# Fifth layer: the bias reaches the rows through the residual instead of through a product

## What is computed

```python
def _sage_conv(x, src, dst, Wl, b, Wr):
    agg = segment_sum(x[src], dst, num_segments=n)
    cnt = segment_sum(ones, dst, num_segments=n)
    mean = agg / jnp.maximum(cnt, 1.0)[:, None]
    return mean @ Wl + b + x @ Wr

x = _layernorm(x + L0(x))    # layers 1 and 2, 128 -> 128 -> 128, relu between
x = _layernorm(x + L1(x))    # layers 3, 4, 5: 128 -> 256 -> 256 -> 128, relu between
```

## Time and profile before

| what | us |
|---|---|
| median of three runs (5212.83 to 5214.96) | 5212.95 |
| the profiled execution, own time | 5213.1 |
| its span | 5211.5 |
| PE busy in the span | 4970.9 (95%) |
| DVE / ACT / POOL busy | 3692.6 / 2554.6 / 2342.6 |
| last pass (b3), first to last bias product | 4032.2 to 5196.4 |

### The profile page before, as it was taken

One profiled execution on the slowest core, in us unless ns is written; L12 is line 12 of the kernel. 1 busy time (PEld: TensorE's weight loads), 2 busy tenths in 40 slices (PEclk: granted clock), 3 DMA queues, 4 the chain that ended last, 5 costly groups with the idle time before them and its releaser, 6 DMA issues. The chain is left out here.

```text
span 5211.5 us, 156564 instructions
## 1 busy us (share of the span) xinstructions
PE 4970.9 (95%) x42398; PEld 4907.3 (94%) x42399; DVE 3692.6 (71%) x10002; ACT 2554.6 (49%) x7254; POOL 2342.6 (45%) x2947
## 2 busy tenths in 40 slices
PE   1899989999998999999899999999998999999999
PEld 0788889999998999999899999999998999999999
DVE  4688877888887999999666666767675555555555
ACT  0455547777774333333333333333333666666666
POOL 1788866666644444444332323222222444444441
PEclk9999999999998999999999999999999999999999
DMA  1677777888875655665555555555555766666665
GB/s 29 172 211 210 208 198 210 229 229 228 229 224 160 196 193 196 197 196 194 167 173 179 173 179 173 178 174 178 174 177 162 222 216 219 219 217 219 219 216 186
DMA packets 1247576, 1007.06 MB, mean 193 GB/s; under 512 B 70406, under 2 KB 1178275, under 8 KB 1247492
## 3 DMA queue, kind: packets, MB, share of 16 engines
q1 hardware_dynamic: 1171780, 825.23, 51.2%
q0 software_dynamic: 75712, 180.76, 11.4%
HBM read 645.58 MB, written 360.13 MB: 193 GB/s over the span
## 5 line engine op out<-in xcount | busy, mean ns | idle before, releaser
L1206 PE MATMUL f_product_b<-f_ring_b,f_onehot_b 128*128 x6272 | 997.2, 281 | 0.0
L1206 PEld LDWEIGHTS f_product_b<-f_ring_b,f_onehot_b 128*128 128x128 f32 x6272 | 856.3, 189 | 0.0
L778 PE MATMUL m_product_a<-m_ring_a,m_onehot_a 128*128 x4704 | 846.9, 291 | 0.0
L1262 ACT ACTIVATE f_ring_b<-f_e_product_b,t_rec_all 128x256 f32 (+1 forms) x784 | 329.4, 471 | 1010.0 <-PE f_e_product_b L1219 1010.0
L1200 PE MATMUL f_product_b<-b_r_all,f_t_hi_b 128*128 128x256 f32 x2352 | 723.1, 307 | 0.0
L901 DVE TENSOR_TENSOR m_onehot_b<-iota_all,t_win_all 128x512 f32<-128x512 f32 x392 | 269.6, 688 | 557.3 <-PE m_product_b L778 557.3
L1202 PE MATMUL f_product_b<-b_r_all,f_t_lo_b 128*128 128x256 f32 x2352 | 661.2, 281 | 0.0
L1201 PE MATMUL f_product_b<-b_r_all,f_t_hi_b 128*128 128x256 f32 x2352 | 659.6, 280 | 0.0
L778 PEld LDWEIGHTS m_product_a<-m_ring_a,m_onehot_a 128*128 128x128 f32 x4704 | 651.9, 192 | 0.0
L1139 POOL TENSOR_TENSOR f_held_b<-ones_all 1x1 f32<-1x1 f32 x390 | 71.5, 183 | 1243.0 <-ACT f_e_idx_b L1244 1152.6
L901 DVE TENSOR_TENSOR m_onehot_a<-iota_all,t_win_all 128x512 fp32r<-128x512 f32 (+1 forms) x784 | 536.8, 686 | 102.7 <-PE m_product_a L778 94.0
(11 more groups left out here) (197 smaller groups left out, 12292.7 us busy)
## 6 DMA issues: line engine op xcount, KB each, us to landing
g<-f_rows_out_b SPq DMA_DIRECT2D x392, 512.0 KB
f_rows_in_b<-g SPq DMA_DIRECT2D x196, 512.0 KB, 4.1
m_rows_in_b<-g SPq DMA_DIRECT2D x196, 512.0 KB
m_t_full_a<-in_x_flat_dram SPq DMA_DIRECT2D x196, 256.0 KB
h<-m_rows_out_a SPq DMA_DIRECT2D x196, 256.0 KB
m_rows_in_a<-h SPq DMA_DIRECT2D x196, 256.0 KB
m_res_in_a<-in_x_dram SPq DMA_DIRECT2D x196, 256.0 KB, 3.1
x<-m_rows_out_a SPq DMA_DIRECT2D x196, 256.0 KB
```

Of the source, the lines that this page charges most:

```text
L778: mm = pe.matmul(both, onehot[:, s, n, :], ring[:, bass.ds(at[n] * (C * fo), C * fo)], start=False, stop=(w == 1), skip_group_check=True)
L1206: mm = pe.matmul(to, onehot[:, s, n, :], ring[:, bass.ds(at[n] * (2 * fo) + half * fo, fo)], start=False, stop=(w == 1 and half == 1))
```

## The change

In the pass of b3 alone (`biased=True`), the bias product is not issued; the first product by Wr of a group carries `start=True`. POOL adds the bias to the residual rows in place, once per group, behind the step's gathers; DVE's `add_up` waits for that addition (new semaphore `s_biased`) instead of for the residual's DMA. The other four passes are as they were.

```diff
@@ pool @@
+            def add_bias(g):
+                s = g.slot(2)
+                wait(pool, res_here[s], g.turn(2) + 1)
+                pool.tensor_tensor(res_in[:, s, :, :], res_in[:, s, :, :],
+                                   cv["bias"][:, :].unsqueeze(1).to_broadcast([P, T, P]),
+                                   ALU.add).then_inc(s_biased.sem, 1)
...
                     gather(p.plus(D))
                 if norm and split and has(g, 1):
                     mix(g.plus(-1))
+                if biased and g is not None:
+                    add_bias(g)
@@ tensor @@
-                    if norm and not split:
+                    if norm and not split and not biased:
                         pe.matmul(product[s][:, :], pr.two_rows[:, :],
...
-                                  start=(not norm and not split and t == 0 and k == 0), stop=False,
+                                  start=(not split and (biased or not norm) and t == 0 and k == 0), stop=False,
@@ vector, add_up @@
-                        wait(v, res_here[s], g.turn(2) + 1)
+                        if biased:
+                            wait(v, s_biased, g.n(1))
+                        else:
+                            wait(v, res_here[s], g.turn(2) + 1)
@@ build @@
-            dict(name="b3", h=g2, out=o2, relu=True, w=2, f_out=128, turned=False, Wl=b_wl3, Wr=b_wr3, b=b_b3,
+            dict(name="b3", h=g2, out=o2, relu=True, w=2, f_out=128, turned=False, biased=True, Wl=b_wl3, Wr=b_wr3, b=b_b3,
```

More of the change, by code:

```diff
@@ L571, in narrow_pass @@
     shared = cv.get("shared", 0)
+    biased = cv.get("biased", False)
     R = 3 if flat is not None else 2
@@ L609, in narrow_pass @@
         names = ("turned", "full", "onehot", "product", "sum", "stats", "meanvar", "std", "rstd", "shift", "normed",
-                 "index", "held", "eturned", "efull", "eproduct", "ring", "ringhi", "part", "mixed", "rest", "eps")
+                 "index", "held", "eturned", "efull", "eproduct", "ring", "ringhi", "part", "mixed", "rest", "biased", "eps")
         (s_turned, s_full, s_onehot, s_product, s_sum, s_stats, s_meanvar, s_std, s_rstd, s_shift, s_normed,
          s_index, s_held, s_eturned, s_efull, s_eproduct, s_ring, s_ringhi, s_part, s_mixed,
-         s_rest, s_eps) = [pr.counter("m_" + x) for x in names]
+         s_rest, s_biased, s_eps) = [pr.counter("m_" + x) for x in names]
         s_done = s_normed if norm else s_sum
@@ L1040, in narrow_pass @@
         s_rest.passed(G)
+    if biased:
+        s_biased.passed(G)
     if norm:
```

## The result

The median fell from 5213.95 to 5171.78 us (4 runs each, 5170.79 to 5172.64 after): ratio 0.9918, 95% interval 0.9901 to 0.9935, 42.2 us less. The prediction said 5170.9. The profiled execution took 5171.59 us with a span of 5169.9.

A forecast was written before the change was run, and what follows sets the result against it. PE was taken to bound the kernel. From the profiled 5213.1 us, 45.1 saved and 3.1 added at the pass's start gave 5171.1, as a median 5170.9 us; the range was 5166 to 5178.

The forecast's parts named there:

- The price of the product: On PE in the last pass: leaving the bias product out saves 0.23 us a step, 45.1 us, between 43 and 47.
- 216 ns: The skill's time for an isolated matmul of 512 columns; the prediction said the trace agrees with it, not the sustained 131 ns.
- The addition: On POOL, once per step: 128x512 values were put at 1.2 us, with bounds of 0.66 and 1.94 us.
- The steady step: POOL holds 4.5 of 5.77 us with the new work, so it costs nothing there and PE does not wait.
- The start: Start of the last pass: POOL has 26 gathers first, so PE waits 2.9 us at group 2; 3.1 us in all.
- I add 0.2 for both: Start of the last pass: 0.2 us for late residual loads behind DVE's sum and ACT's late copy of edge rows.
- The rows of group 4: Residual load behind DVE's late first sum: lands at 4051.2 to 4051.7, PE wants it at 4051.6, a tie.
- Rival 1: PE's clock falls in the new gap at the pass's start, losing 3 to 5 us: 5174 to 5176; chance 0.15.
- Rival 2: The bias product was partly overlapped on PE, at 131 ns, so the time is 5190 us; chance 0.03.
- rival 3: A wait at the first product by Wr replaces the saving, 0.23 us idle a step: 5216 us; chance 0.04.
- Rival 4: POOL's serial list becomes the bound, deciding from an addition of 2.5 us; at 3.5 us, 5360 us; chance 0.04.
- if POOL's idle time is gone: A sign in the profile after that would show the prediction wrong; it expected idle time still ahead of each POOL marker.

## Why the prediction was right

- **The price of the product**: 0.23 us a step and 45.1 us were forecast; leaving it out (with the addition gone) measured 45.2 us, doubling it 45.8. The reading of starts, not durations, carried it: the duration, 476 ns, would have said 93 us. The stated error of 43 to 47 us was too narrow: two distances of starts are subtracted and one of them is doubled, so 0.01 us in each start can add up to 0.06 us a step, 12 us in all.
- **The figure of 131 ns for a sustained matmul of 512 columns** from the Trainium skill, TensorE: Matmul & The Clock Gate, section on the back-to-back issue gap, does not hold here: a second such matmul put right behind the first adds 0.234 us a step. The prediction's reason for preferring the section's 216 ns, a distance of 0.31 us to the next start, fits neither figure; the price of 0.231 to 0.234 us is what lies near it.
- **The addition**: 1.2 us from IOTA's slope, 1.28 measured. The factor of two of the Trainium skill (GPSIMD Engine Reference, engine selection) agrees, 1.28 to DVE's 0.66, and changed nothing, since POOL had the room. The steady step cost nothing, as forecast: the pass has 1168.0 us with and without the addition where the product is kept, and 1122.9 and 1122.8 us where it is gone.
- **The start**: the mechanism, its place and its order were right; the size was not: 3.1 us forecast, 4.3 measured on that chip (1127.1 - 1122.8). PE's wait for the sum lengthened that step by 3.4 instead of 2.9 us: POOL's addition took 0.07 longer, from its end to PE's product it was 0.94 us instead of the sum's 0.7, and the rest is PE being early against POOL. The term most out is "I add 0.2 for both", the loads behind the late sum, which came to 0.9. The rows of group 4 were 0.5 late, not tied. The 4.1 us of the earlier trace rows are those of another pass's load (f_rows_in); from the issue of this one at 4046.28 to PE's transposes it was 5.04 us. The rows of group 5 cost another 0.5, and they were not in the forecast at all. Two things came together there. DVE's compare at 4047.55 took 1.98 us because it met the second addition, which made the second sum and the loads behind it some 0.5 late; and the load itself, issued at 4050.64, took 6.9 us, 1.36 of them for the issue. Either alone would by these numbers have cost little or nothing.
- **Rival 1** (clock) did not occur: 1.00 in the stretch with the wait. Rival 2 (partial overlap) fell with the doubled product, and rival 3 (a wait in place of the product) with PE's step of 5.78 us without a gap.
- **Rival 4** (POOL's bound) was sized wrongly, without effect on the number: "3.27 us plus the addition. It decides from 2.5 us on". The 3.27 held a meeting that gives way; with 2.70 the point is near 3.0 us, and two additions (2.64 us in all) cost nothing. Its last sign of being wrong, "if POOL's idle time is gone", was too strong for the same reason: with two additions that time is gone, and PE loses nothing.
- That the total came so near is in part luck. The pass gave 40.9 us where 42.0 were forecast. But its first product also came 1.1 us earlier in the profile after, which the edit doesn't explain, and the end behind the last product took 0.4 us longer, so the two profiled spans differ by 41.6. A single execution's earlier passes move by that much.
- What the prediction did not say: that the start's cost depends on how long the opening takes on the chip. Where PE and ACT go through it slowly, POOL is ahead and the cost is nil. On the second chip the pass is 1168.0 - 1122.9 = 45.1 us shorter, the whole price of the product; the medians there differ by 45.6.

## What to carry to other kernels

Price a matmul on a dense PE by the distance of starts around it, against the same pair of neighbours without it. An engine that has idle time in the steady step may have none at the start of a pass: before you give it work, walk its list from the pass's first instruction to the new one. Before an edit goes from one pass to the next, compare the partner's idle time too, and not just the engine that receives the work: here the same edit gained 41 to 45 us in a pass of 6.0 us steps and lost some 76 in one of 4.0.

## What was not expected of the hardware

- A DVE compare, whose two inputs lie in on-chip memory, and POOL's addition do not share time: the compare took 1.98 us beside an addition of 1.29, and 1.94 in the second layer, its 0.69 plus the whole addition. The reverse holds as well: POOL's second addition was 1.76 instead of 1.28, a marker of one element 0.67 instead of 0.18, and a gather that starts beside a compare 1.30 instead of 1.03. A gather that had begun 0.42 us ahead of the compare kept its 1.03. DVE's reciprocal beside the second addition (4606.95) kept its 0.17. The Trainium skill, GPSIMD Engine Reference, names this contention for DVE instructions with two such inputs in its section on specifications; the trace agrees. The price here is the length of the other instruction, as far as the two overlap.
- These meetings are elastic. With two additions POOL's list slid against DVE's until they met where there was room, so a busy time read with meetings in it (3.27 us) overstated what the list needs (2.70).
- The same program differs between chips: 5214 us on the first, 5337 to 5375 on the others, with the opening of the last pass 15 us on one and 25 to 29 on the rest. The profile shows PE and ACT waiting without a releaser there; what holds them stays open.
